# Turning the routed experts' rows with a transposing DMA in place of TensorE

## What is computed

```python
B, S, D, E, H, K = (4, 256, 256, 8, 512, 2)
gate_scores = x @ Wg + bg
_, idx = jax.lax.top_k(gate_scores, K)
mask = jax.nn.one_hot(idx, E, dtype=x.dtype).sum(axis=-2)
h = jax.nn.gelu(jnp.einsum('td,edh->teh', xf, W1) + b1[None], approximate=False)
y = jnp.einsum('teh,ehd->ted', h, W2) + b2[None]
out = jnp.einsum('ted,te->td', y, mf)
```

## Time and profile before

| | us |
|---|---|
| median of 3 runs | 1183.03 |
| lowest, highest | 1182.34, 1183.16 |
| span of the profiled execution | 1182.9 |
| this stage's tiles on GpSimd (tile 0 to tile 27 starts) | 476.10 to 668.13 |
| first transposes of the next stage | 674.80 |

### The profile page before, as it was taken

How to read it: one execution, slowest core, us unless ns; L and a number is a source line. 1 busy time by engine, 2 the same in 40 slices (tenths; PEclk the granted TensorE clock), 3 DMA queues, 4 the chain that set the end, 5 groups by cost and what they waited for, 6 DMA issues and landing times. The chain is left out here.

```text
span 1182.9 us, 22185 instructions
## 1 busy us (share of the span) xinstructions
PE 1135.1 (96%) x8024; PEld 853.5 (72%) x8024; DVE 563.3 (48%) x1532; ACT 361.8 (31%) x697; POOL 168.6 (14%) x160
## 2 busy tenths in 40 slices
PE   5989999999999997999999699999999999999998
PEld 4667777776668886888888577555566688866765
DVE  8888888834447677111111363000044355248654
ACT  5764554422211102333333333100022201044333
POOL 3300000000000456444445300000000000001000
PEclk9999999999999998999999799999999999999999
DMA  6610000047532446456664521120066445135101
GB/s 194 211 44 13 25 25 12 25 127 180 160 102 91 134 131 186 67 116 145 121 151 76 124 89 45 49 83 32 17 160 186 136 131 162 58 98 179 44 22 42
DMA packets 134097, 118.16 MB, mean 100 GB/s; under 512 B 23030, under 2 KB 122105, under 8 KB 134016
## 3 DMA queue, kind: packets, MB, share of 16 engines
q1 hardware_dynamic: 103392, 77.67, 22.8%
q0 software_dynamic: 12448, 18.95, 8.1%
q10 hardware_dynamic: 18176, 20.45, 5.1%
HBM read 67.34 MB, written 49.29 MB: 99 GB/s over the span
## 5 line engine op out<-in xcount | busy, mean ns | idle before, releaser
L1364 PE MATMUL b_pa<-adj,l_parts 128*128 (+2 forms) x980 | 141.7, 296 | 0.4 <-ACT adj L1295 0.4
L1364 PEld LDWEIGHTS b_pa<-adj,l_parts 128*128 128x128 f16 x980 | 91.2, 97 | 29.5 <-issue 0.5
L2907 POOL DMA_INDIRECT x<-ring,l_row_i x56 | 87.4, 1561 | 113.1 <-DMA x<-ring,l_row_i 75.5
L2714 PE MATMUL l_sum<-l_parts,ring 128*128 128x256 f32 x448 | 101.6, 380 | 0.2 <-ACT ring L2811 0.2
L1605 DVE SCALAR_TENSOR_TENSOR l_parts<-dense,scale,l_parts 128x256 f16<-128x256 f32 x48 | 23.2, 483 | 158.2 <-ACT l_parts L1596 158.2
L1572 PE MATMUL dense<-room,ring 128*128 128x512 f32 x200 | 93.9, 593 | 0.2 <-ACT ring L1553 0.2
L2714 PEld LDWEIGHTS l_sum<-l_parts,ring 128*128 128x128 f32 x448 | 83.0, 190 | 10.9 <-ACT ring L2811 0.4
L2290 PE MATMUL l_sum<-l_parts,adj 128*128 128x256 f16 x735 | 82.9, 273 | 1.2 <-DVE rows L2018 1.2
L2290 PE MATMUL l1b_sum<-l_parts,adj 128*128 128x256 f16 x735 | 82.9, 273 | 0.9 <-DVE rows L2018 0.9
L2290 PEld LDWEIGHTS l_sum<-l_parts,adj 128*128 128x128 f16 x735 | 71.2, 98 | 10.7 <-issue 2.7
L2290 PEld LDWEIGHTS l1b_sum<-l_parts,adj 128*128 128x128 f16 x735 | 71.4, 98 | 10.4 <-issue 2.4
(11 more groups left out here) (471 smaller groups left out, 1879.5 us busy)
## 6 DMA issues: line engine op xcount, KB each, us to landing
ring<-sums_and_zt SPq DMA_DIRECT2D x50, 256.0 KB, 3.4
l_expert_xr<-slots_in SPq DMA_DIRECT2D x28, 257.0 KB
l_parts<-in_L_ffn_W SPq DMA_DIRECT2D x12, 512.0 KB, 5.2
pre<-room ACTq DMA_DIRECT2D x34, 128.0 KB, 2.1
sums_and_zt<-ring SPq DMA_DIRECT2D x10, 320.0 KB, 2.3
ring<-inv SPq DMA_DIRECT2D x50, 64.0 KB, 4.0
sums_and_zt<-room ACTq DMA_DIRECT2D x5, 640.0 KB, 3.6
adj<-xt SPq DMA_DIRECT2D x5, 640.0 KB, 4.5
```

Source lines behind the costliest of these rows:

```text
L1364: ins = nc.tensor.matmul(pa[f][:, 0:size], parts[:, k, a, f * P:(f + 1) * P], adj[:, k, ds(r * BW, size)], start=k == 0 and a == 0, stop=k ...
L2714: ins = nc.tensor.matmul(to[t], h[:, n, t * P:(t + 1) * P], w2[:, u, n, :], start=i == 0, stop=i == HB - 1)
L2907: pool.indirect_dma_start(out=g["x1"], in_=y[:, half, t, :], in_offset=None, compute_op=ALU.add, out_offset=bass.IndirectOffsetOnAxis(ap=i ...
```

## The change

For tiles 10 to 27, TensorE's four transposes are gone, as is ScalarE's eviction of them. Tile 9, the first of expert 2, and all tiles of experts 0 and 1 are as before.

- VectorE (`split`) copies the loaded rows as 16-bit words into two planes, the low halves of each float32 and the high halves (two copies of 128 x 512 words), and takes the row numbers (a third copy), which ScalarE did before. This stands inside `one_tile` of tile j, for tile j + 2, between the two additions of L2858, behind a wait for `flipped` of tile j + 1 and a wait for the rows of tile j + 2.
- SyncE issues one `dma_start_transpose` per tile (128 x 1024 16-bit words, SBUF to SBUF, 256 KB) from `planes` to `flipped`. Ahead of it, it waits until VectorE has split the tile and until ScalarE has taken the tile before. The load of the next rows comes behind it, and the register load of its address between the two.
- ScalarE (`take_flipped`) joins the planes into `xt` with two copies of 128 x 512 words, behind the GELUs of the tile before.
- The loops over experts 2 to 7 on ScalarE and VectorE are written out, and the last two tiles stand by themselves on VectorE. The first weights of the next layer wait for ScalarE to have taken the last tile.

`planes` and `flipped` lie in `room`, and that is what the rows of the order call them.

```diff
     ids_now = tile["ids_now"]
+    planes = work.room[:, 0:NT * D].bitcast(U16)
+    flipped = work.room[:, NT * D:2 * NT * D].bitcast(U16)
+    plane = lambda a: planes.rearrange("p (t a d) -> p t a d", t=NT, a=2)[:, :, a, :]
+    words = lambda ap, a: ap.bitcast(U16).rearrange("p t (d a) -> p t d a", a=2)[:, :, :, a]
...
@@ -2609,6 +2613,19 @@
 
         return (eng.value_load(g["tiles"][0:1, 0, ds(e, 1)], min_val=1, max_val=STMAX),
                 eng.value_load(g["tiles"][0:1, 1, ds(e, 1)], min_val=0, max_val=STMAX - 1))
+
+    def start_on(eng, e):
+
+        return eng.value_load(g["tiles"][0:1, 1, e:e + 1], min_val=e, max_val=STMAX - LAST_MOST - (E0 - 1 - e))
+
+    def end_on(eng, e):
+
+        return start_on(eng, e + 1) if e < E0 - 1 else total_on(eng)
+
+    def from_end(eng, n):
+
+        at = len(FIRST_ROWS) - n
+        return eng.value_load(g["from"][0:1, at:at + 1], min_val=E0 + LAST_MOST - 1 - n, max_val=STMAX - n)
 
     def later_range(eng, e, tiles):
 
@@ -2635,12 +2652,14 @@
         load_first_layer(sp, io, weights, 0, 0, table.s["first_w1_in0"])
         scattered(sp, range(SETTLED))
         load_rows(sp, 0)
+        sp.sem_inc(s["flipped"], 16)
 
     def sync(sp):
         def load(j, at):
             sp.wait_ge(s["turned"], j)
             sp.wait_ge(s["ids_ready"], j)
             load_rows(sp, at)
+            sp.sem_inc(s["flipped"], 16)
 
         def load_from_table(j):
             load(j, sp.value_load(g["from"][0:1, ds(j, 1)], min_val=0, max_val=LAST_ROW))
@@ -2655,11 +2674,12 @@
         later_tiles(sp, 0, load_from_table)
         later_tiles(sp, 1, load_from_table)
         def range_on(e):
-            return (tiles_on(sp, e)[1], sp.value_load(g["tiles"][0:1, 2, ds(e, 1)], min_val=2, max_val=STMAX - (e < E0 - 1)),
+            return (start_on(sp, e), end_on(sp, e),
                     sp.value_load(table.cnt_i[0:1, 0, ds(e, 1)], min_val=FIXED, max_val=E0 - 1))
 
         following = range_on(2)
-        load_from_table(following[0])
+        second = following[0]
+        load_from_table(second)
         for e in range(2, E0):
             u = e % 2
             at, end, which = following
@@ -2667,8 +2687,18 @@
             load_expert(sp, io, weights, which, u, s[f"w_in{u}"])
             if e < E0 - 1:
                 following = range_on(e + 1)
+            if e == 2:
+                sp.wait_ge(s["turned"], sp.snap(second + 1))
+                sp.wait_ge(s["ids_ready"], sp.snap(second + 1))
+                sp.sem_inc(s["planes_ready"], 1)
             with sp.Fori(at, end if e < E0 - 1 else sp.snap(end - 1)) as j:
-                load_from_table(sp.snap(j + 1))
+                load_rows(sp, sp.value_load(g["from"][0:1, ds(sp.snap(j + 1), 1)], min_val=0, max_val=LAST_ROW))
+                sp.wait_ge(s["ids_ready"], sp.snap(j + 2))
+                sp.wait_ge(s["xt_ready"], sp.snap(j + 1))
+                sp.sem_inc(s["planes_ready"], 1)
+                sp.dma_start_transpose(flipped.rearrange("p (c r) -> p c r", r=P), planes).then_inc(s["flipped"], 16)
+        total = total_on(sp)
+        sp.wait_ge(s["xt_ready"], total)
         work.load_first_weights(sp, first, s["first_in"])
         for n, (t, count) in enumerate(FIRST_ROWS):
             settled = sp.value_load(g["from"][0:1, n:n + 1], min_val=E0 + LAST_MOST - 3 + n, max_val=STMAX - 2 + n)
@@ -2720,8 +2750,9 @@
             pe.wait_ge(s["y_done"], NT * before)
             multiply_h(u, halves, before)
 
-        def step(j, u):
-            turn(j)
+        def step(j, u, turned=False):
+            if not turned:
+                turn(j)
             second_product(j, u)
             first_product(j, u)
 
@@ -2758,16 +2789,16 @@
 
         def expert(e, u, uses):
             tiles, at = tiles_on(pe, e)
-            turn(at)
             if e > 2:
                 second_product(at, 1 - u)
             else:
+                turn(at)
                 second_product_left(at)
             pe.wait_ge(s[f"w_in{u}"], LOADS * uses)
             first_product(at, u)
             with pe.If(tiles > 1):
                 with pe.Fori(1, tiles) as i:
-                    step(pe.snap(at + i), u)
+                    step(pe.snap(at + i), u, turned=True)
             with pe.Else():
                 pe.nop()
 
@@ -2815,11 +2846,22 @@
             take_rows(act, j, px)
             take_products(j, u)
 
-        def expert(e, u):
-            _, at = tiles_on(act, e)
-            end = act.value_load(g["tiles"][0:1, 2, ds(e, 1)], min_val=1, max_val=STMAX)
-            with act.Fori(at, end) as j:
-                one_tile(j, u)
+        def take_flipped(j):
+
+            act.wait_ge(s["flipped"], 16 * (j + 1))
+            for a in range(2):
+                ins = nc.scalar.activation(words(xt, a).rearrange("p k (t n) -> p k t n", t=NT),
+                                           flipped.rearrange("p (t a k n) -> p a k t n", t=NT, a=2, k=KD)[:, a], ACT.Copy)
+            ins.then_inc(s["xt_ready"], 1)
+
+        def expert(e, second):
+            u = e % 2
+            at, end = second if e == 2 else start_on(act, e), end_on(act, e)
+            with act.Fori(at, end if e < E0 - 1 else act.snap(end - 1)) as j:
+                take_products(j, u)
+                take_flipped(act.snap(j + 1))
+            if e == E0 - 1:
+                take_products(from_end(act, 1), u)
 
         act.sem_inc(s["h_done"], HB)
         scattered(act, [SETTLED])
@@ -2830,9 +2872,10 @@
         act.wait_ge(table.s["tables_ready"], 1)
         later_tiles(act, 0, lambda j: one_tile(j, 0))
         later_tiles(act, 1, lambda j: one_tile(j, 1))
-        with act.Fori(1, E0 // 2) as k:
-            expert(k * 2, 0)
-            expert(k * 2 + 1, 1)
+        second = start_on(act, 2)
+        take_rows(act, second, px)
+        for e in range(2, E0):
+            expert(e, second)
         small, w2_size = work.first_small, KD * D
         act.wait_ge(s["first_in"], FIRST_LOADS)
         nc.scalar.activation(work.first_w2, work.first_w2, ACT.Square, accum_out=small[:, 0, 1:2]).then_inc(s["squared"], 1)
@@ -2845,7 +2888,15 @@
         act.wait_ge(s["rooted"], 1)
 
     def vector(dve):
-        def one_tile(j, u, products=halves):
+        def split(j):
+
+            dve.wait_ge(s["rows_in"], 16 * (j + 1))
+            for a in range(2):
+                nc.vector.tensor_copy(plane(a), words(xr[:, :, 0:D], a))
+            nc.vector.tensor_copy(ids[:, ds(j, 1), :].rearrange("p a t -> p (a t)"), xr[:, :, D:DW].rearrange("p t a -> p (t a)")
+                                  ).then_inc(s["ids_ready"], 1)
+
+        def one_tile(j, u, products=halves, ahead=False):
             flat = lambda ap: ap[:, ds(j, 1), :].rearrange("p a t -> p (a t)")
             half = ds(j % 2, 1) if isinstance(j, int) else ds(dve.snap(j & 1), 1)
             if not isinstance(j, int) or j >= 2:
@@ -2857,12 +2908,19 @@
                 dve.wait_ge(s["y_mm"], NT * j + (t + 1 if products is halves else NT))
                 nc.vector.tensor_tensor(y[:, half, t, :].rearrange("p a d -> p (a d)"), products[t],
                                         b2[:, u, :], ALU.add).then_inc(s["y_done"], 1)
-
-        def expert(e, u):
+                if ahead and t == 0:
+                    dve.wait_ge(s["flipped"], 16 * (j + 2))
+                    split(dve.snap(j + 2))
+
+        def expert(e):
+            u = e % 2
             tiles, at = tiles_on(dve, e)
-            end = dve.value_load(g["tiles"][0:1, 2, ds(e, 1)], min_val=1, max_val=STMAX)
-            with dve.Fori(at, end) as j:
-                one_tile(j, u)
+            end = end_on(dve, e)
+            with dve.Fori(at, end if e < E0 - 1 else dve.snap(end - 2)) as j:
+                one_tile(j, u, ahead=True)
+            if e == E0 - 1:
+                one_tile(from_end(dve, 2), u)
+                one_tile(from_end(dve, 1), u)
             dve.wait_ge(s["y_done"], NT * (at + tiles + 1))
             dve.sem_inc(s[f"w_free{u}"], 1)
 
@@ -2878,9 +2936,11 @@
             tiles, at = tiles_on(dve, e)
             dve.wait_ge(s["y_done"], NT * (at + tiles + 2 - e))
             dve.sem_inc(s[f"w_free{e}"], 1)
-        with dve.Fori(1, E0 // 2) as k:
-            expert(k * 2, 0)
-            expert(k * 2 + 1, 1)
+        second = start_on(dve, 2)
+        dve.wait_ge(s["ids_ready"], dve.snap(second + 1))
+        split(dve.snap(second + 1))
+        for e in range(2, E0):
+            expert(e)
```

4 lines of the change are left out of this document (2 added, 2 removed).

## The result

The changed kernel takes 1207.23 us (1206.19 to 1210.82 in four runs) where the kernel before takes 1182.68 in the same runs: a ratio of 1.0216, 95% interval 1.0198 to 1.0234, so 24.5 us slower. The forecast of 1200 had the sign, and its range held the time, but the cost is 24.5 us where 17 were expected. Every median in what follows is over all runs of a kernel, every ratio over its fast runs alone; two variants of the kernel before each have one run far outside the rest (2404.91 and 1338.97 us).

The account below looks back on a forecast made before the run. GpSimd's chain of accumulations was taken to bound the stage, with TensorE nearly as full. Steps of 7.76 us (13) and 8.90 us (5) made 145.4 against 127.74, +17.7 us: 1200 us, range 1177 to 1240.

Parts of the forecast that it names:

- The bound: GpSimd's accumulating DMAs set the stage's end; the 7.7 us taken from TensorE count 0.
- The traffic beside the accumulations: Transposing DMA and row load beside GpSimd's accumulations: 0.63 us each, 1.26 us per step without weights.
- the sum: GpSimd's 18 steps from tile 9 to 27: 145.4 us against 127.74, so +17.7 us.
- SyncE's order: Weights and row loads queued behind the transposing DMA on SyncE: cost 0, up to 10 us for the range.
- GpSimd's slack: At five changes of expert, about 4 us on GpSimd would take in a split 3 to 4 us late.
- The split on VectorE: Two copies of 0.5 us, 1.2 with the third; hidden if the transposing DMA is back in time.
- The sign that was named: GpSimd's steps over 7.10 us, each released by its own DMAs; landings over 3.8; quiet-step DMA share well over 0.5.
- ScalarE: One eviction of 0.60 us goes, two copies totalling 1.2 us come; cost 0 as work.
- the new DMA is the bound: Rival: the transposing DMA's own time sets GpSimd's step, mostly 1203 to 1260 us; chance 0.24.
- D: Transposing DMA's time from issue to landing: taken as 4.5 us, bounds 3.4 and 13.0, deciding from 5.3.
- Hidden: Rival: accumulations keep their pace and TensorE's gain lies under GpSimd's chain, 1183.0 us; chance 0.15.
- faster: Rival: fewer weights and row loads fall on GpSimd's wait; all steps at 6.50 give 1172.3 us; chance 0.19.

Follow-up runs that it names:

- early weights: Changed kernel with the next expert's weights issued in the last pass over an expert's tiles, ahead of the transposing DMA: 1199.55 us.
- one-block DMA: Kernel with early weights, its transposing DMA moving one 128 x 128 block in place of eight for experts 3 to 7: 1184.66 us.
- held idle DMA: Kernel before plus 18 unread transposing DMAs, held on SyncE until the result two tiles before is whole, weights ahead of the wait: 1194.74 us.
- rows first: Changed kernel with SyncE's next row load moved ahead of the transposing DMA in the loop over an expert's tiles: 1201.67 us.

## Why the prediction held, and where it failed

- **The bound.** Right. TensorE's saving is worth nothing at the end (one transpose in place of four: 1183.15), because GpSimd's chain of accumulations sets it. The second chain, TensorE's, is nearly as full, as the prediction had it: with half of the accumulations gone the kernel gains 4.0 us, and then TensorE's tile of 7.33 us sets the step.
- **The traffic beside the accumulations.** The mechanism was right, and the size near: 1.26 us a quiet step was forecast, 0.8 to 1.1 were measured with early weights (7.3 to 7.6 against 6.50), 0.17 of it GpSimd's own slower DMA. Over the stage, tile 27 starts 14.5 us later than before with early weights (682.58, in the fastest of four runs), where the sum had 17.7. Of the shares one was right: the transposing DMA alone costs 0.56 to 0.64 (7.06 and 7.31 - 0.17), just the 0.63 taken for it. The other was too large: the row load, also taken at 0.63, costs between nothing (beside the one-block DMA, 4.1 us after the start; beside the held idle DMA, 4.6) and about 0.3 (with early weights, 4.65). The price came from two steps whose releaser was "issue", not a landing; a row that doesn't name the landing cannot price it. A third step with a row load at the same point, 4.62 us after the start of tile 17, was in the same trace, was released by a landing, and took 6.65 us (599.24 to 605.89): 0.15 over the quiet one. That the sum is near is in part luck, since GpSimd's slower DMA, which it did not have, made up for some of the row load's excess.
- **The step that failed: SyncE's order, costed at 0.** One change of it gave back 7.7 us. The prediction had the weights' 7 us against TensorE's 7; TensorE stood still 4.13 us at the change shown, 17.1 us at all five, and then ran at a lower clock. It had the split 3 to 4 us late and gave that to GpSimd's slack. But the split stands ahead of the second addition on VectorE, so the slack was not there: GpSimd's second DMA was late by part of the same wait (3.62 us after the first, not 1.86). Counted against the kernel before of the same runs each time, the difference is 24.5 - 16.5 = 8.0 us. The 10 us that were kept for it at the upper end cover it. With early weights 16.5 us are left, near the 17.7 of the sum.
- **The split on VectorE, called hidden.** It was short enough (two copies of 0.43 us where 0.5 was taken), but hidden only while rows are there. In the quiet step shown it cost GpSimd's second DMA 0.6 us; put behind the second addition, it gained nothing for the kernel.
- **The sign that was named.** Steps longer than 7.10, landings later than 3.8 us (4.0, and 4.4 with early weights), a DMA share well over 0.5: all there. But not every start was released by its own DMAs: of GpSimd's waits 11 ended with VectorE's addition, and VectorE waited for rows, not for the transposing DMA, a case that the prediction didn't name. The profile of the changed kernel alone would have allowed the reading that the new waits are everything; only the variant without them showed the 16.5 us below.
- **ScalarE.** Two copies of 0.77 us where 0.60 was taken. TensorE waited for them (4.2 us in the changed kernel, 12.5 with early weights), but with early weights none of that reached GpSimd.
- **The rival "the new DMA is the bound"** fell: D is 3.7 us, under the 4.5 taken and the 5.3 from which it decides. The estimate of 10.5 us for eight blocks, from the 1309 ns a block of the Trainium skill, "VectorE: DVE Perf Modes", section "The three transpose paths", did not come out: eight blocks landed in 3.7 us, so that figure does not add up over the blocks of one DMA. The Trainium skill, "Advanced Engine Details and Errata", section "X-Bar Transpose (TRN2)", has transposing DMAs as fast as regular ones; here the landing took 3.9 us in the median against 2.8 for the plain DMA with early weights, so the trace does not agree.
- **"Hidden" and "faster"** fell with the term of the traffic. "Hidden" would have been close if the DMA had lain 4 us or more behind GpSimd's start (1186.67).

Open is why a transposing DMA delays the accumulations more than a plain one of the same bytes. The page of the profile counts 1056 small packets for it; that the packets are the reason was not tried. Open is also how the 7.7 us divide between late weights and late rows, since the variant with rows first scattered too much to tell.

## What to carry to other kernels

Ask of an added DMA not only how many bytes it moves and whether it is back in time, but whose landing it runs beside: the same idle DMA cost 3 us in one place of the step and 12 in another. And put no load that others need soon behind a DMA that waits for other work; moving the weights out from behind it gave back a third of the loss here. Two such changes need not add up: rows first and weights early together gave 1.1 us, less than either alone. Before work is taken off an engine that is busy 96% of the time, take it off without putting anything in its place: here that variant said that the work was worth nothing.

## What the runs showed of the hardware

- A transposing DMA of 256 KB within SBUF takes SyncE 1.32 us to issue in the median, a plain one of the same size 0.47; it lands in 3.7 to 3.9 us against 2.8, and counts as 1056 packets under 512 bytes.
- It lengthened the step of an accumulating pair of indirect DMAs, 6.50 us, by about 0.6 us when issued 1.5 to 1.9 us after the first of them, and by 0.2 or less when issued 4.1 to 5.8 us after it or, in one case, 0.16. A plain DMA of the same bytes, issued 1.83 us after it, left the step at 6.65 in the one case without a row load.
- GpSimd's indirect DMA took 1.73 us in place of 1.56 in most steps with early weights, beside VectorE's 16-bit copies, and 1.56 to 1.58 for each of tiles 9 to 27 in the kernels without such copies.
- A 16-bit copy of 128 x 512 words with a stride of two on one side took VectorE 0.43 us and ScalarE 0.77.
- After 4.13 us of idling TensorE's granted clock was 0.68 in the mean of the next 5.3 us, and 1.00 after that.
